# Graph layer on one core: one release for a chunk's gathers, two scatter matmuls, a transposed product tile, five key blocks on ScalarE

## The chip, the cores and the metric

The kernel runs on one core of a Trainium2 chip. The metric is device time in microseconds (us) of one execution. Three runs of the kernel before gave 1787.23, 1787.67 and 1792.86 us; their median is 1787.67 us. The engines are called as in the profile: PE is TensorE, DVE is VectorE, ACT is ScalarE, POOL is GpSimd, SP is SyncE, which issues most loads.

## The reference

One message-passing layer on a graph of 6250 nodes with 64 features and 206250 edges, sorted by destination. In short:

```python
h = maximum(layernorm(x), 0)
msg = relu(h[src] + edge_attr)                    # one row of 64 per edge
agg = segment_sum(msg, dst, 6250)
out = x + relu((h + agg) @ W1 + b1) @ W2 + b2
```

All is float32. The costly part is h[src], a gather of 206250 rows of 256 bytes, and the sum of the edges by destination.

## The kernel before

**Tiling.** The edges are cut into 124 chunks of 13 tiles of 128 edges (`TILES_PER_CHUNK` = 13). A partition holds 13 neighbouring edges of a chunk, and since edges are sorted, each partition's edges mostly have one or two destinations. Four chunks make a turn; there are 31 turns (t, with u = 0 to 3 for the chunk in it) and four sets of buffers (`SLOTS`). Turn 0 and the last three turns (`EARLY_TURNS`, 28 to 30) are written out; turns 1 to 27 are a loop on each engine, each engine with its own.

**Two ways to fetch h[src].** Of a chunk's 13 tiles, nine are fetched by POOL: `gather_rows` issues one indirect DMA a tile from `h_table` in DRAM (L361). The other four are made by PE (`pe_tiles`): `candidates` multiplies, for each tile, a one-hot matrix of keys (`keyhot`, seven key blocks) with the table of h, kept as two float16 halves. That is 14 matmuls of 128x448 a tile (L1050), into one of four PSUM banks, and it yields seven candidate rows for each edge. DVE masks them (L820) and sums over the seven (L826); this is `combine`.

**The keys.** The one-hot matrix of a chunk has seven key blocks. DVE makes `DVE_BLOCKS` = 3 of them (L710) and ACT four, each with an Abs (L617) and then one Relu over all four (L621). There are two `keyhot` buffers, so those of a chunk can be made once PE is done with the chunk two before it.

**The sum by destination.** For each chunk DVE runs three steps, laid between the masks of the following chunk (`segment_step`): `sum_edges` adds the gathered rows to the edge rows that ACT copied to PSUM (L856); `part_edges` applies relu and multiplies with a flag for each edge, once for the destination of the partition's first edge and once for that of its last (L865, 2 x 13 x 64 elements, into `parts`); `add_parts` sums over the 13 tiles (L875) into `ends`, two rows of 64 a partition. `scatter_ends` on PE multiplies these with a one-hot matrix of the place in a window of 64 nodes (L385), each end in two matmuls of 32 columns, and DVE adds the window to `agg` (L897). A float32 matmul shows as two records in the trace.

**Order and releases.** PE does two chunks of candidates and then the scatters of two earlier chunks. In the loop POOL gathers chunk c while PE makes the candidates of chunk c-2, and is held to its pace: `gather_chunk` passes `gather_rows` a list of releases, and before gathers 0, 2, 4 and 6 of a chunk POOL waits for the first, second, third and fourth candidate tile of chunk c-2:

```python
gather_rows(u, n, gathered[u], {i * n // m: pe_before(old_t, old_u, i) + 1 for i in range(m)})
```

Before that it waits for the chunk's indices and until `sum_edges` has read the buffer's former rows. SP loads keys, indices and edges for two chunks at a time, one pair ahead (`load_pair`); the edge loads (L492) mark the pairs in the trace. At the end `first_layer` and `second_layer` run the two dense layers (L411, L426) on finished groups of nodes.

Of the kernel before, what the change touches and what calls it, by code (L numbers as in the profile page):

```python
# [13 lines left out]
P = 128  # L14
D = 64
# [23 lines left out]
WIN = 64  # L39
AGG_COLS = MARGIN + NODES_PAD + WIN  # L40
BLOCK = 64
QUARTER = 32
ENDS = 2
SEGMENT_STEPS = 3
N_BLOCKS = NODES_PAD // BLOCK
# [36 lines left out]
assert PE_FIRST[-1] == PE_TILES[-1] and PE_MAX == max(*PE_FIRST, *PE_LAST[0], *PE_LAST[1], *PE_LAST[2])  # L82
CAND = GROUP
KEY_BLOCKS = N_GROUPS
DVE_BLOCKS = 3
CAND_BANKS = 4
F16 = mybir.dt.float16
BF16 = mybir.dt.bfloat16
# [78 lines left out]
def build(nc, x_rows, x_cols, src_t, src_keys, src_cands, dst_t, base_t, edges_t, w1, b1, w2, b2, out):  # L167
# [8 lines left out]
    with ExitStack() as ctx:  # L176
# [52 lines left out]
        edge = [edge_pair[u // PAIR][:, u % PAIR, :, :] for u in range(SLOTS)]  # L229
        gath = [sb(f"gath{u}", [P, TILES_PER_CHUNK, D]) for u in range(SLOTS)]  # L230

        parts = sb("parts", [P, ENDS, TILES_PER_CHUNK, D])
        msg = parts[:, 0, :, :]
        ends = [sb(f"ends{u}", [P, ENDS, D]) for u in range(SLOTS)]

        onehot = [sb(f"onehot{u}", [P, ENDS, WIN]) for u in range(SLOTS)]
# [118 lines left out]
        def gather_rows(u, tiles, signal, released=None):  # L355

            for r in range(tiles):
                if released is not None and r in released:
                    nc.gpsimd.wait_ge(cands_ready, released[r])
                    nc.gpsimd.sem_inc(slot_taken, 1)  # L360
                nc.gpsimd.indirect_dma_start(  # L361
                    out=gath[u][:, r, :], out_offset=None, in_=h_table,
                    in_offset=bass.IndirectOffsetOnAxis(ap=idx[u][:, r:r + 1], axis=0),
                ).then_inc(signal, 16)
# [16 lines left out]

        def scatter_ends(u, bank, signal):
            for k in range(ENDS):
                for d in range(0, D, QUARTER):
                    last = nc.tensor.matmul(bank[k * D + d:k * D + d + QUARTER, 0:WIN],  # L385
                                            ends[u][:, k, d:d + QUARTER], onehot[u][:, k, :], start=True, stop=True)
            last.then_inc(signal, 1)

        def scatter_strays(bank, signal):
# [130 lines left out]
        @block.gpsimd  # L520
        def _(pool):
            nc.gpsimd.iota(iota_i[:, :], [[1, P]], base=0, channel_multiplier=0).then_inc(iota_made, 1)
            nc.gpsimd.iota(iota_p[:, :], [[0, 1]], base=0, channel_multiplier=1).then_inc(iota_made, 1)

            nc.gpsimd.iota(key_iota_i[:, :], [[P, KEY_BLOCKS]], base=0, channel_multiplier=1).then_inc(iota_made, 1)

            pool.wait_ge(iota_made, 3)
            nc.gpsimd.memset(agg[D:2 * D, :], 0.0).then_inc(odd_half_zeroed, 1)  # L530
            pool.wait_ge(odd_half_zeroed, 1)

            for g in POOL_CENTRES:
                pool.wait_ge(mean_ready, g + 1)
                centre(nc.gpsimd, g).then_inc(centred_by_pool, 1)


            pool.wait_ge(h_stored, 16 * N_GROUPS)
            for u in range(SLOTS):
                pool.wait_ge(idx_loaded[u // PAIR], 16)  # L540
                gather_rows(u, pool_tiles(0, u), gathered[u])

            def gather_chunk(t, u):
                pool.wait_ge(idx_loaded[u // PAIR], t * 16 + 16)

                pool.wait_ge(summed, t * SLOTS + (u + 1 - SLOTS))

                old_t, old_u = back(t, u, 2)
                n, m = pool_tiles(t, u), pe_tiles(old_t, old_u)
                gather_rows(u, n, gathered[u], {i * n // m: pe_before(old_t, old_u, i) + 1 for i in range(m)})  # L550

            with pool.Fori(1, EARLY_TURNS[0]) as t:
                for u in range(SLOTS):
                    gather_chunk(t, u)
            for t in EARLY_TURNS:
                for u in range(SLOTS):
                    gather_chunk(t, u)

            pool.wait_ge(flag_ready, 1)
            flag = pool.value_load(outside_i[0:1, 0:1], min_val=0, max_val=P)  # L560
            with pool.If(flag > 0):
                with pool.Fori(0, N_CHUNKS) as c:
                    pool.wait_ge(g_free, c + 1)
                    pool.wait_ge(g_idx_loaded, c * 16 + 16)
                    pool.sem_inc(slot_taken, 1)
                    gather_rows(0, TILES_PER_CHUNK, g_gathered)
# [105 lines left out]
        def _(dve):  # L672
# [186 lines left out]
            def part_edges(t, u):  # L859

                dve.wait_ge(summed, t * SLOTS + u + 1)
                if u > 0 or not first(t):

                    dve.wait_ge(ends_ready, t * SLOTS + u)
                nc.vector.scalar_tensor_tensor(  # L865
                    out=parts[:, :, :, :],
                    in0=(edge_near if near(t) else edge_sum).unsqueeze(1).to_broadcast([P, ENDS, TILES_PER_CHUNK, D]),
                    scalar=0.0,
                    in1=side[:, bass.ds(t * SLOTS + u, 1), :, :].rearrange("p c k r -> p (c k) r").unsqueeze(3)
                    .to_broadcast([P, ENDS, TILES_PER_CHUNK, D]), op0=ALU.max, op1=ALU.mult).then_inc(parted, 1)  # L870

            def add_parts(t, u):

                dve.wait_ge(parted, t * SLOTS + u + 1)
                nc.vector.tensor_reduce(ends[u][:, :, :], parts[:, :, :, :].rearrange("p k r d -> p k d r"), AX_X,  # L875
                                        ALU.add).then_inc(ends_ready, 1)

            def segment_step(step, t, u):
                if step == 0:
# [298 lines left out]
```

## Time and profile before

| What | Value |
|---|---|
| Median of three runs | 1787.67 us |
| Profiled execution, its own time | 1790.81 us |
| Its span | 1789.0 us |
| Mean granted clock of TensorE | 0.922 |
| PE busy | 1500.4 us (84%) |
| DVE busy | 1450.7 us (81%) |
| ACT busy | 667.0 us (37%) |
| POOL busy | 1101.1 us (62%), 1125 gathers |
| DMA | mean 64 GB/s |

The page gives the busy time of each engine, the chain of work that ended last, and the groups of instructions by line. The timeline gives single instructions in order, with the idle time before them in brackets and what ended it. "issue" there means that the engine waited for nothing that the profile shows, "remote" another core or a queue that it doesn't know. Matmuls are pipelined: what counts is the distance from start to start. "DMA_INDIRECT" on POOL is the making of one gather's descriptors, not the transfer.

### The profile page before, as it was taken

Reading aid. Unit: us, or ns where it says so; the run is one execution under the profiler, and the core shown is the slowest. Engines: PE = TensorE matmul, PEld = TensorE weight load, DVE = VectorE, ACT = ScalarE, POOL = GpSimd, SP = SyncE. Lnnn points to the kernel's source line nnn. Section 1 sums busy time; section 2 is a strip of 40 time slices with the busy share of each in tenths; the row PEclk is TensorE's granted clock in tenths of the full one; section 3 lists DMA queues with packets and bytes.
Section 4 is the critical chain, followed back from the end, with each engine's and each line's share of the span. In section 5 each row is a group of like instructions: output and inputs, shape, how many; then the busy total and the mean of one; then the engine's idle time right before and its main releaser. Section 6 shows DMA issues by size and latency. Waiting matters only on the chain.

```text
span 1789.0 us, 25748 instructions
## 1 busy us (share of the span) xinstructions
PE 1500.4 (84%) x7987; PEld 729.6 (41%) x7987; DVE 1450.7 (81%) x2075; ACT 667.0 (37%) x759; POOL 1101.1 (62%) x1136
## 2 busy tenths in 40 slices
PE   4498898889888988988888989889889889889675
PEld 2143444344444434434444444444444344444332
DVE  8299888878878878888888888888888787889565
ACT  5033433343344334334433433344344334333221
POOL 4566666666666666666666566666666665667660
PEclk9699999999899999999999989999999899999796
DMA  5122222221221222212212212212222222122120
GB/s 202 25 72 49 70 72 58 61 71 48 72 71 48 72 70 49 72 48 71 72 48 72 71 47 72 71 48 72 64 55 72 48 72 71 47 72 74 45 59 21
DMA packets 67162, 115.15 MB, mean 64 GB/s; under 512 B 29810, under 2 KB 32882, under 8 KB 67010
## 3 DMA queue, kind: packets, MB, share of 16 engines
q1 hardware_dynamic: 30130, 75.86, 12.7%
q0 software_dynamic: 36000, 36.94, 10.6%
q10 hardware_dynamic: 1008, 2.06, 0.3%
q8 instruction: 12, 0.20, 0.0%
q14 instruction: 12, 0.10, 0.0%
HBM read 111.43 MB, written 3.34 MB: 64 GB/s over the span
## 4 chain that ended last, share of the span: by engine, by line
PE 66%; issue 15%; DVE 13%; another core or an unknown queue 4%; DVEq 1%; ACT 1%; POOL 0%; POOLq 0%
PE ps_cand L1050 63%; DVE picked L820 3%; DVE gath L826 3%; DVE ends L875 2%; DVE parts L865 2%; PE ps L385 2%; DVE keyhot L710 1%; PE ps_edge L411 1%; ACT agg L601 0%; DVEq L887 0%; PE ps_edge L426 0%; DVE key_iota L687 0%; DVE cand_mask L758 0%; DVE side L774 0%
## 5 line engine op out<-in xcount | busy, mean ns | idle before, releaser
L361 POOL DMA_INDIRECT gath<-h_table,idx_pair x1125 | 1092.3, 971 | 640.8 <-issue 328.1
L1050 PE MATMUL ps_cand<-table_hi,keyhot 128*128 128x448 f16 x3409 | 1252.0, 367 | 85.6 <-issue 78.1
L1050 PE MATMUL ps_cand<-table_lo,keyhot 128*128 128x448 f16 x3409 | 1250.0, 367 | 79.0 <-issue 78.5
L1050 PEld LDWEIGHTS ps_cand<-table_hi,keyhot 128*128 128x128 f16 x3409 | 344.0, 101 | 459.3 <-issue 170.4
L1050 PEld LDWEIGHTS ps_cand<-table_lo,keyhot 128*128 128x128 f16 x3409 | 343.9, 101 | 425.1 <-issue 149.7
L820 DVE TENSOR_TENSOR picked<-ps_cand,cand_mask 128x448 f32<-128x448 f32 x487 | 300.9, 618 | 265.0 <-remote 179.1
L608 ACT ACTIVATE ps_edge<-edge_pair 128x832 f32<-128x832 f32 x112 | 97.4, 869 | 799.7 <-DVE parts L865 559.7
L875 DVE TENSOR_REDUCE ends<-parts 128x128 f32<-128x1664 f32 x124 | 372.9, 3007 | 0.0
L617 ACT ACTIVATE keyhot<-key_pair,key_bias 128x512 f16<-128x512 f16 (+2 forms) x480 | 302.9, 702 | 182.0 <-remote 113.2
L826 DVE TENSOR_REDUCE gath<-picked 128x64 f32<-128x448 f32 x487 | 298.1, 612 | 4.1
L621 ACT ACTIVATE keyhot<-keyhot,hot_bias 128x2048 f16<-128x2048 f16 (+2 forms) x120 | 236.8, 1974 | 3.9
L865 DVE SCALAR_TENSOR_TENSOR parts<-ps_edge,side 128x1664 f32<-128x1664 f32 x112 | 210.6, 1881 | 0.7 <-issue 0.7
L710 DVE TENSOR_SCALAR keyhot<-key_pair,key_iota 128x512 f16<-128x512 f16 (+2 forms) x388 | 117.2, 359 | 0.2
L856 DVE TENSOR_TENSOR ps_edge<-gath,ps_edge 128x832 f32<-128x832 f32 x112 | 114.0, 1018 | 0.0
L385 PE MATMUL ps<-onehot,ends 128*32 128x64 f32 x992 | 48.6, 237 | 56.6 <-issue 55.3
L385 PEld LDWEIGHTS ps<-onehot,ends 128*32 128x32 f32 x992 | 26.4, 113 | 95.3 <-issue 91.6
L897 DVE TENSOR_TENSOR agg<-agg,ps 128x64 f32 x124 | 27.0, 217 | 42.0 <-DVE agg L897 22.1
L417 ACT ACTIVATE xh<-ps_edge,b_sb 64x448 f32<-64x448 f32 (+2 forms) x14 | 8.8, 629 | 116.6 <-PE ps_edge L411 108.3
L411 PE MATMUL ps_edge<-agg,w_sb 128*64 128x448 f32 (+2 forms) x28 | 19.6, 800 | 38.1 <-DVE x_sq L436 15.0
L838 DVE TENSOR_TENSOR onehot<-iota_f,place 128x128 f32<-128x128 f32 x124 | 35.2, 284 | 9.5 <-remote 7.4
L1025 PE MATMUL ps<-ident,xh 128*64 128x128 f32 x49 | 11.7, 417 | 26.1 <-DVE xh L741 21.7
L865 DVE SCALAR_TENSOR_TENSOR parts<-xh,side 128x1664 f32<-128x1664 f32 x12 | 22.6, 1880 | 0.0
(71 smaller groups left out, 156.9 us busy)
## 6 DMA issues: line engine op xcount, KB each, us to landing
edge_pair<-edges_t SPq DMA_DIRECT2D x62, 832.0 KB
gath<-h_table,idx_pair POOLq DMA_INDIRECT x1125
key_pair<-key_table SPq DMA_DIRECT2D x62, 256.0 KB
h_table<-xh SPq DMA_DIRECT2D x7, 224.0 KB, 2.5
x_b<-x_cols SPq DMA_DIRECT2D x1, 1568.0 KB
out<-x_sq SPq DMA_DIRECT2D x6, 224.0 KB
idx_pair<-src_t SPq DMA_DIRECT2D x62, 13.0 KB
xh<-x_rows ACTq DMA_DIRECT2D x4, 224.0 KB, 5.2
```

The costliest lines, as they stand in the source:

```text
L361: nc.gpsimd.indirect_dma_start(out=gath[u][:, r, :], out_offset=None, in_=h_table, in_offset=bass.IndirectOffsetOnAxis(ap=idx[u][:, r:r + ...
L385: last = nc.tensor.matmul(bank[k * D + d:k * D + d + QUARTER, 0:WIN], ends[u][:, k, d:d + QUARTER], onehot[u][:, k, :], start=True, stop=True)
L608: nc.scalar.activation(edge_near, edge[u], ACT.Copy).then_inc(edge_copied, 1)
L617: last = nc.scalar.activation(keyhot[u % 2][:, a, 0:n], key[u][:, P * PE_MAX - n:], ACT.Abs, bias=key_bias[:, a:a + 1])
L621: nc.scalar.activation(keyhot[u % 2][:, DVE_BLOCKS:, 0:n], keyhot[u % 2][:, DVE_BLOCKS:, 0:n], ACT.Relu, bias=hot_bias[:, 0:1], scale=-1.0 ...
L710: last = nc.vector.tensor_scalar(keyhot[u % 2][:, a, 0:n], key[u][:, P * PE_MAX - n:], key_iota[:, a:a + 1], 1.0 / SCALE, ALU.is_equal, AL ...
L820: nc.vector.tensor_tensor(picked[i][:, :, :], ps_cand[buf][:, 0:D * CAND].rearrange("p (d b) -> p d b", b=CAND), mask.to_broadcast([P, D, ...
L826: nc.vector.tensor_reduce(gath[u][:, pool_tiles(t, u) + i, :], picked[i][:, :, :], AX_X, ALU.add).then_inc(selected, 1)
L856: nc.vector.tensor_tensor(edge_near if near(t) else edge_sum, gath[u][:, :, :], edge_near if near(t) else edge[u], ALU.add).then_inc(summe ...
L865: nc.vector.scalar_tensor_tensor(out=parts[:, :, :, :], in0=(edge_near if near(t) else edge_sum).unsqueeze(1).to_broadcast([P, ENDS, TILES ...
L875: nc.vector.tensor_reduce(ends[u][:, :, :], parts[:, :, :, :].rearrange("p k r d -> p k d r"), AX_X, ALU.add).then_inc(ends_ready, 1)
L1050: last = nc.tensor.matmul(bank[:, 0:D * CAND], keyhot[u % 2][:, a, i * P:(i + 1) * P], half[:, a, :, :].rearrange("p d b -> p (d b)"), sta ...
```

## The change

Four things change. In `gather_rows` POOL waits only in front of gather 0 of a chunk, for the first candidate tile of chunk c-2; the three other waits and their increments of `slot_taken` go. `scatter_ends` issues one matmul of 64 columns for each end in place of two of 32. `parts` is laid out with the 13 tiles innermost, so `add_parts` reads contiguous elements; `part_edges` becomes two instructions, one for each end, each writing its elements 13 words apart. `DVE_BLOCKS` falls from 3 to 2, so ACT makes five key blocks.

```diff
--- before.py
+++ after.py
@@ -39,7 +39,6 @@
 WIN = 64
 AGG_COLS = MARGIN + NODES_PAD + WIN
 BLOCK = 64
-QUARTER = 32
 ENDS = 2
 SEGMENT_STEPS = 3
 N_BLOCKS = NODES_PAD // BLOCK
@@ -82,7 +81,7 @@
 assert PE_FIRST[-1] == PE_TILES[-1] and PE_MAX == max(*PE_FIRST, *PE_LAST[0], *PE_LAST[1], *PE_LAST[2])
 CAND = GROUP
 KEY_BLOCKS = N_GROUPS
-DVE_BLOCKS = 3
+DVE_BLOCKS = 2
 CAND_BANKS = 4
 F16 = mybir.dt.float16
 BF16 = mybir.dt.bfloat16
@@ -229,8 +228,8 @@
         edge = [edge_pair[u // PAIR][:, u % PAIR, :, :] for u in range(SLOTS)]
         gath = [sb(f"gath{u}", [P, TILES_PER_CHUNK, D]) for u in range(SLOTS)]
 
-        parts = sb("parts", [P, ENDS, TILES_PER_CHUNK, D])
-        msg = parts[:, 0, :, :]
+        parts = sb("parts", [P, ENDS, D, TILES_PER_CHUNK])
+        msg = parts[:, 0, :, :].rearrange("p d r -> p (d r)").rearrange("p (r d) -> p r d", d=D)
         ends = [sb(f"ends{u}", [P, ENDS, D]) for u in range(SLOTS)]
 
         onehot = [sb(f"onehot{u}", [P, ENDS, WIN]) for u in range(SLOTS)]
@@ -355,8 +354,8 @@
         def gather_rows(u, tiles, signal, released=None):
 
             for r in range(tiles):
-                if released is not None and r in released:
-                    nc.gpsimd.wait_ge(cands_ready, released[r])
+                if released is not None and r == 0:
+                    nc.gpsimd.wait_ge(cands_ready, released)
                     nc.gpsimd.sem_inc(slot_taken, 1)
                 nc.gpsimd.indirect_dma_start(
                     out=gath[u][:, r, :], out_offset=None, in_=h_table,
@@ -381,9 +380,8 @@
 
         def scatter_ends(u, bank, signal):
             for k in range(ENDS):
-                for d in range(0, D, QUARTER):
-                    last = nc.tensor.matmul(bank[k * D + d:k * D + d + QUARTER, 0:WIN],
-                                            ends[u][:, k, d:d + QUARTER], onehot[u][:, k, :], start=True, stop=True)
+                last = nc.tensor.matmul(bank[k * D:(k + 1) * D, 0:WIN], ends[u][:, k, :], onehot[u][:, k, :],
+                                        start=True, stop=True)
             last.then_inc(signal, 1)
 
         def scatter_strays(bank, signal):
@@ -546,8 +544,7 @@
                 pool.wait_ge(summed, t * SLOTS + (u + 1 - SLOTS))
 
                 old_t, old_u = back(t, u, 2)
-                n, m = pool_tiles(t, u), pe_tiles(old_t, old_u)
-                gather_rows(u, n, gathered[u], {i * n // m: pe_before(old_t, old_u, i) + 1 for i in range(m)})
+                gather_rows(u, pool_tiles(t, u), gathered[u], pe_before(old_t, old_u) + 1)
 
             with pool.Fori(1, EARLY_TURNS[0]) as t:
                 for u in range(SLOTS):
@@ -862,18 +859,18 @@
                 if u > 0 or not first(t):
 
                     dve.wait_ge(ends_ready, t * SLOTS + u)
-                nc.vector.scalar_tensor_tensor(
-                    out=parts[:, :, :, :],
-                    in0=(edge_near if near(t) else edge_sum).unsqueeze(1).to_broadcast([P, ENDS, TILES_PER_CHUNK, D]),
-                    scalar=0.0,
-                    in1=side[:, bass.ds(t * SLOTS + u, 1), :, :].rearrange("p c k r -> p (c k) r").unsqueeze(3)
-                    .to_broadcast([P, ENDS, TILES_PER_CHUNK, D]), op0=ALU.max, op1=ALU.mult).then_inc(parted, 1)
+                for k in range(ENDS):
+                    last = nc.vector.scalar_tensor_tensor(
+                        out=parts[:, k, :, :].rearrange("p d r -> p r d"), in0=edge_near if near(t) else edge_sum,
+                        scalar=0.0,
+                        in1=side[:, bass.ds(t * SLOTS + u, 1), k, :].rearrange("p c r -> p (c r)").unsqueeze(2)
+                        .to_broadcast([P, TILES_PER_CHUNK, D]), op0=ALU.max, op1=ALU.mult)
+                last.then_inc(parted, 1)
 
             def add_parts(t, u):
 
                 dve.wait_ge(parted, t * SLOTS + u + 1)
-                nc.vector.tensor_reduce(ends[u][:, :, :], parts[:, :, :, :].rearrange("p k r d -> p k d r"), AX_X,
-                                        ALU.add).then_inc(ends_ready, 1)
+                nc.vector.tensor_reduce(ends[u][:, :, :], parts[:, :, :, :], AX_X, ALU.add).then_inc(ends_ready, 1)
 
             def segment_step(step, t, u):
                 if step == 0:
```

## Rows read from the trace of the kernel before

**Rows 1.** The page, part 4: the chain of waits, by engine and by line.
```profile
PE 66%; issue 15%; DVE 13%; another core or an unknown queue 4%; DVEq 1%; ACT 1%; POOL 0%; POOLq 0%
PE ps_cand L1050 63%; DVE picked L820 3%; DVE gath L826 3%; DVE ends L875 2%; DVE parts L865 2%; PE ps L385 2%; DVE keyhot L710 1%; PE ps_edge L411 1%; ACT agg L601 0%; DVEq L887 0%; PE ps_edge L426 0%; DVE key_iota L687 0%; DVE cand_mask L758 0%; DVE side L774 0%
```

**Rows 2.** Timeline of SP: start us, us, engine, line, operation: edge loads.
```profile
102.27 0.33 SPq L492 DMA_DIRECT2D edge_pair<-edges_t  x1
...
1565.67 0.33 SPq L492 DMA_DIRECT2D edge_pair<-edges_t  x1
```

**Rows 3.** Timeline of PE around one stall; in brackets idle before, releaser.
```profile
813.74 0.35 PE L1050 MATMUL ps_cand<-table_hi,keyhot 128*128 128x448 f16 x1
813.93 0.35 PE L1050 MATMUL ps_cand<-table_lo,keyhot 128*128 128x448 f16 x1
...
815.99 0.35 PE L1050 MATMUL ps_cand<-table_lo,keyhot 128*128 128x448 f16 x1 [1.08 <-issue]
817.40 0.35 PE L1050 MATMUL ps_cand<-table_hi,keyhot 128*128 128x448 f16 x1 [1.06 <-issue]
818.10 0.54 PE L1050 MATMUL ps_cand<-table_lo,keyhot 128*128 128x448 f16 x1 [0.36 <-issue]
818.43 0.58 PE L1050 MATMUL ps_cand<-table_hi,keyhot 128*128 128x448 f16 x1
818.81 0.58 PE L1050 MATMUL ps_cand<-table_lo,keyhot 128*128 128x448 f16 x1
```

**Rows 4.** Timeline of PE: a scatter slot, and a second layer.
```profile
791.93 0.43 PE L385 MATMUL ps<-onehot,ends 128*32 128x64 f32 x16
792.29 0.36 PE L1050 MATMUL ps_cand<-table_hi,keyhot 128*128 128x448 f16 x1
...
1714.05 1.67 PE L426 MATMUL ps_edge<-w_sb,xh 65*128 65x64 f32 x14
```

**Rows 5.** Timeline of POOL: first and last gathers of two runs.
```profile
788.84 0.95 POOL L361 DMA_INDIRECT gath<-h_table,idx_pair  x1 [2.64 <-remote]
...
802.51 0.94 POOL L361 DMA_INDIRECT gath<-h_table,idx_pair  x1 [2.60 <-remote]
...
815.03 0.94 POOL L361 DMA_INDIRECT gath<-h_table,idx_pair  x1 [0.30 <-issue]
818.96 0.94 POOL L361 DMA_INDIRECT gath<-h_table,idx_pair  x1 [2.99 <-remote]
```

**Rows 6.** Timeline of PE and POOL at the start.
```profile
48.39 0.35 PE L1050 MATMUL ps_cand<-table_hi,keyhot 128*128 128x448 f16 x1 [0.18 <-issue]
...
74.92 0.95 POOL L361 DMA_INDIRECT gath<-h_table,idx_pair  x1 [0.30 <-issue]
...
79.19 0.53 PE L1050 MATMUL ps_cand<-table_lo,keyhot 128*128 128x448 f16 x1 [0.87 <-issue]
```

**Rows 7.** Waits: who waited for whom: us, times, longest us.
```profile
POOL gath L361 <- PE ps_cand L1050: 160.5, 84, 16.6
PE ps_cand L1050 <- issue: 156.5, 189, 2.5
POOL gath L361 <- remote: 140.7, 57, 3.6
```

**Rows 8.** Groups by shape: xcount, busy us, mean ns, idle before.
```profile
L875 DVE TENSOR_REDUCE ends<-parts 128x128 f32<-128x1664 f32 x124 | 372.9, 3007 | 0.0
L826 DVE TENSOR_REDUCE gath<-picked 128x64 f32<-128x448 f32 x487 | 298.1, 612 | 4.1
L617 ACT ACTIVATE keyhot<-key_pair,key_bias 128x512 f16<-128x512 f16 x456 | 291.0, 709 | 170.9 <-remote 113.2 <-PE ps_cand L1050 42.9 <-issue 14.7
L621 ACT ACTIVATE keyhot<-keyhot,hot_bias 128x2048 f16<-128x2048 f16 x114 | 228.2, 2002 | 3.7
L865 DVE SCALAR_TENSOR_TENSOR parts<-ps_edge,side 128x1664 f32<-128x1664 f32 x112 | 210.6, 1881 | 0.7 <-issue 0.7
L710 DVE TENSOR_SCALAR keyhot<-key_pair,key_iota 128x512 f16<-128x512 f16 x363 | 110.9, 362 | 0.2
```

## Prediction

> **What bounds the kernel now.** I read the chain of waits first. It shows TensorE (PE) holding 66% of the path, nearly all of it the candidate matmuls of L1050, and 15% as "issue", time in which PE waits for nothing that the profile names [rows 1]. So the question is how fast PE walks through its matmuls. The loop over turns 1 to 27 handles 54 pairs of chunks, and the edge loads on SP mark them: (1565.67 - 102.27) / 54 = 27.10 us a pair [rows 2]. A pair needs 112 candidate matmuls at 0.19 us start to start (813.74 to 813.93 [rows 3]), 21.2 us, and one slot of 0.36 us for its scatters (791.93 to 792.29 [rows 4]): 21.5 us. The missing 5.6 us are the "issue" time and the slow clock behind it.
>
> The timeline says where they come from. At 813.93 PE stops running at 0.19 us and takes 1.4 us a matmul (815.99, 817.40), with no semaphore named; at 818.10 it runs again, and its matmuls come 0.38 us apart for a while (818.43, 818.81), the pace of 1.2 GHz in place of 2.4, before they are fast again [rows 3]. Beside it stands GpSimd (POOL): it had issued eleven gathers 1.25 us apart without a break from 802.51, the last at 815.03, and then stood for 2.99 us until 818.96 [rows 5]. PE began to starve 11.4 us after that run began and recovered 2.1 us after its last gather ended (815.97 to 818.10). This repeats: I count 28 unbroken runs of eleven gathers and six of thirteen, nearly all with a stall of PE that ends 2.0 to 2.4 us after the run does. 32 runs have nine; the one at 788.84 is followed by a break of 2.6 us. The plainest case is at the start, where no wait ties the two. POOL issues 37 gathers without a break until 75.87; PE falls to 1.4 us a matmul from 48.39, with all its operands there, and runs on at 79.19 [rows 6]. So a long unbroken run of gathers starves PE of instructions, and only a break of POOL ends it.
>
> The breaks are made by the waits in gather_rows. POOL stood 160.5 us for PE's candidates by name and 140.7 us for "remote" [rows 7]; by position in a chunk, in turns 1 to 27, I get 53 us in front of gather 0 and 71, 91 and 41 us in front of gathers 2, 4 and 6, which the change takes away.
>
> The Trainium skill ("Runtime: NRT & Kernel Launch", "Instruction fetch mechanics") says that the sequencer fetches instructions over its own DMA queue in blocks and that this is mostly hidden. By that rule a run of gathers would do nothing to PE and the gathers' term would be 0, a sum of 1781 us or, with fewer PE instructions, the rival "faster" below. The trace disagrees with "hidden": PE stood with nothing named for 156.5 us in front of the candidate matmuls alone [rows 7].
>
> **The gathers at one release.** Chunk c waits once, for the first candidate tile of chunk c-2, and then issues nine gathers in 9 x 1.25 = 11.25 us. The next release comes when PE has done another 56 matmuls and half a scatter slot, 56 x 0.189 + 0.2 = 10.8 us if it isn't starved. Starvation starts about 11.4 us into a run. So a chunk's nine gathers end just after the next release is there, and POOL goes on without a break. Today it is caught at gather 2, whose release needs 14 matmuls more (13.4 us), so the run ends at eleven. After the change nothing stops it before the eighteenth, whose successor needs a release PE is far from. One cycle, from one run's start to the next, for two chunks (112 + 8 = 120 matmul records, since a pair's scatters fall from 16 to 8):
> - The run takes 17 x 1.25 + 0.95 = 22.2 us; PE is fed again at 22.2 + 2.1 = 24.3 us.
> - Fed stretch: I take 11.9 us instead of 11.4, as PE passes some 5% fewer instructions. (11.9 - 0.36) / 0.189 = 61 records.
> - Starved stretch: 24.3 - 11.9 = 12.4 us at 1.41 us = 9 records. (At the start it was as slow, or slower.)
> - Rest: 50 records, eight at 0.374 us on the slow clock and 42 at 0.189 us: 10.9 us, in which POOL stands.
> Together 35.2 us against 27.10: +8.1 us a pair. With PE fed the whole break, the next run finds it in the same state, so the pattern should hold. I let 48 of 54 pairs do it (the first turns run behind VectorE, and a run now and then will be broken after nine): 48 x 8.1 = +389 us. Bounds: in the timeline the stalls start between 9.3 us (run from 1301.5, after a short break) and 12.8 us (run from 873.2) into a run. With 9.3: 47 + 11 records by 24.3 us, 62 left, 13.2 us, so 37.5 us a pair, +10.4, times 54 = +562 us. With 12.8: 66 + 8, 46 left, 10.2 us, 34.5 us a pair, +7.4 a pair; if only half of the pairs do it, +200 us. Unrolled turns 28 to 30: POOL has gathers of 2.5 us among its own there, I take 0.
>
> **Two scatter matmuls of 64 columns.** Now 16 records of a pair share a slot of 0.36 us. Seven second-layer matmuls, full width, make 14 records in 1.67 us, 0.107 us each [rows 4], so the narrow ones run beside each other. Afterwards eight records are twice as wide. If they run two abreast the slot stays 0.4 us; one by one, 8 x 0.107 = 0.86 us, +0.5 us x 62 = +31 us; if the slot halves, -11 us. Nearest row is today's overlap: 0.
>
> **VectorE.** The sum over r (L875) takes 3.007 us for 1664 elements read 64 apart; L826 sums 448 contiguous ones in 0.612, and L865 passes 1664 in 1.881 [rows 8]. Between the last two lie 1.04 ns an element and 0.144 us fixed, so the contiguous sum is 1.88 us: -1.13 us a chunk. The product becomes two of 832 elements, 0.144 + 0.868 = 1.01 us each, +0.14 together, if writing 13 words apart costs nothing; at L875's slope, (3.007 - 0.144) / 1664 = 1.72 ns, they take 2 x 1.57 = 3.15 us, +1.27. One key block less: -0.30 us (L710 takes 0.362, the next starts 0.3 later). VectorE's sum: -1.3 to -0.2 us a chunk. It lies beside PE. L875 has only 2% of the path [rows 1], 36 us, of which 1.13 / 3.007 = 38% could go: 13 us, where VectorE leads at the start and in turns 28 on. I take -10; the bounds are -13 and 0.
> The Trainium skill ("Advanced Engine Details and Errata", "Memory Cachelines") says SBUF has 16-byte lines and an access that changes line each time pays. The 3.007 us of L875 agree. Applied to the new write, 52 bytes apart, it makes VectorE's gain close to nothing: the term would be 0 and the sum 10 us higher.
>
> **ScalarE.** One more key block, 0.61 of its 0.709 us, and a Relu over 2560 instead of 2048 elements, 2.002 x 1.25: +1.1 us a chunk [rows 8]. A chunk of ScalarE now takes 5.3 us (a copy of 0.87, four blocks of 0.61, the Relu of 2.0); at 13.5 us a chunk the rest is idle, and its keys are there some 4 to 9 us before PE turns to them. 0; if that cover were gone, 124 x 1.1 = +136 us.
>
> **Sum.** Profiled execution: span 1789.0, time 1790.8 us, 3.1 us over the median of 1787.67. 1790.8 + 389 + 0 - 10 + 0 = 2170; on the scale of the median 2167, say 2165 us.
>
> **Rivals.**
> - Half of it. Runs of nine stay where PE starves before the next release; today's 32 such runs speak for it, and a pair costs 27.1 us then. Against it: fewer PE instructions make the stall start later, and after a long break PE is full. With 24 of 54 pairs in runs of eighteen: +194 - 10, 1970 us.
> - Faster: the breaks of POOL are only the effect of PE's stall, which has its own cause in PE's instruction count. Then the change costs nothing on POOL and PE passes 496 of 7987 matmul records fewer, 6%. Stalls and the slow clock behind them take 5.6 x 54 = 302 us; 6% is 19 us, and VectorE's 10 more: 1760 us. It decides if POOL's run does not set the end of a stall. For it: the stall frees POOL's own wait. Against: the fixed 2.1 us behind the last gather, and 37 gathers at the start with no wait in between.
> - No change: POOL's saved breaks come back as one longer break before gather 0, as long in sum, with stalls as today and VectorE's gain hidden: 1788 us.
> - That the change doesn't do what it says: the 54 pairs could run with breaks at gather 0 of 2 to 3 us each, as at 788.84 to 802.51, 13.7 us a chunk. This is the case of no change again.
>
> **Chances.** Runs of eighteen in most pairs, 2165 us: 0.62, own range 2060 to 2270. Half of it, 1970: 0.19. Faster, 1760: 0.12. No change: 0.04. The remaining 0.03 is a small loss, 1800 to 1880, by scatters in single file or wide writes. A measurement tells a change of 0.3% (5 us). Faster 0.12, same 0.04, slower 0.84. The range from 1880 to 2280 us leaves out the two small cases and the far ends.
>
> **What would show it.** Right: runs of eighteen gathers 1.25 us apart, breaks of some 12 us before gather 0 and none elsewhere; PE at 1.4 us a matmul for 10 to 13 us in each pair, ending 2 us after a run; edge loads 35 us apart; PE's mean granted clock below today's. The scatter slot at 0.4 us; L875 at 1.9 us; the two products at 1.0 us each if the write is free, 1.6 if not. Wrong: PE at 0.19 us a matmul in the second half of a run of eighteen, or pairs at 27 us with runs of nine.

## The result and the profile after

The changed kernel takes 1872.24 us (median of four runs, 1865.08 to 1887.71) against 1787.61 us for the kernel before (four runs, 1787.23 to 1792.86): ratio 1.047, 95% interval 1.0441 to 1.05. It is slower, as forecast, but by 85 us and not by 377, and outside the range. ("Fed" means below that PE's matmuls start 0.19 us apart, or 0.38 at the slow clock; "starved" that they start 1.4 to 2.8 us apart with no wait named.) The profiled execution has a span of 1863.1 us, its own time is 1865.08 us, and TensorE's mean granted clock is 0.905 (before 0.922).

The page after, part 4, the chain of waits: PE and "issue" hold 89% of it, 81% before [rows 1].

```profile
PE 72%; issue 17%; DVE 8%; another core or an unknown queue 2%; ACT 1%; DVEq 0%; POOL 0%; POOLq 0%
```

Timeline of SP after, the edge loads that answer to [rows 2]:

```profile
102.01 0.33 SPq L490 DMA_DIRECT2D edge_pair<-edges_t  x1
...
1640.76 0.33 SPq L490 DMA_DIRECT2D edge_pair<-edges_t  x1
```

(1640.76 - 102.01) / 54 = 28.50 us a pair, against 27.10. The loop costs 54 x 1.40 = 75 us more, the start and the end together 1 us less: all of the profiled execution's 74 us lies in the loop.

Timeline of POOL after: first and last gather of a run of nine, then the same of a run of eighteen, then the next run.

```profile
844.64 0.94 POOL L360 DMA_INDIRECT gath<-h_table,idx_pair  x1 [2.85 <-PE ps_cand L1047]
...
854.63 0.94 POOL L360 DMA_INDIRECT gath<-h_table,idx_pair  x1 [0.30 <-issue]
858.21 0.94 POOL L360 DMA_INDIRECT gath<-h_table,idx_pair  x1 [2.64 <-remote]
...
879.49 0.94 POOL L360 DMA_INDIRECT gath<-h_table,idx_pair  x1 [0.30 <-issue]
889.58 0.95 POOL L360 DMA_INDIRECT gath<-h_table,idx_pair  x1 [9.15 <-PE ps_cand L1047]
```

Timeline of PE beside that run of eighteen, which answers to [rows 3] and [rows 4]:

```profile
838.34 0.35 PE L1047 MATMUL ps_cand<-table_lo,keyhot 128*128 128x448 f16 x1
...
860.85 0.45 PE L383 MATMUL ps<-onehot,ends 128*64 128x64 f32 x8
861.23 0.36 PE L1047 MATMUL ps_cand<-table_hi,keyhot 128*128 128x448 f16 x1
...
869.95 0.35 PE L1047 MATMUL ps_cand<-table_hi,keyhot 128*128 128x448 f16 x1
870.25 0.35 PE L1047 MATMUL ps_cand<-table_lo,keyhot 128*128 128x448 f16 x1
872.35 0.35 PE L1047 MATMUL ps_cand<-table_hi,keyhot 128*128 128x448 f16 x1 [1.75 <-issue]
875.16 0.53 PE L1047 MATMUL ps_cand<-table_lo,keyhot 128*128 128x448 f16 x1 [2.46 <-issue]
...
882.16 0.53 PE L1047 MATMUL ps_cand<-table_hi,keyhot 128*128 128x448 f16 x1 [1.57 <-issue]
883.57 0.55 PE L1047 MATMUL ps_cand<-table_lo,keyhot 128*128 128x448 f16 x1 [0.87 <-issue]
883.91 0.58 PE L1047 MATMUL ps_cand<-table_hi,keyhot 128*128 128x448 f16 x1
...
888.44 0.35 PE L1047 MATMUL ps_cand<-table_lo,keyhot 128*128 128x448 f16 x1
```

The stall is the one forecast: it begins 12.0 us after the run (870.25 against 858.21) and ends 3.1 us after the last gather (883.57 against 880.43). In it PE passes one matmul every 1.4 to 2.8 us. All 18 runs of eighteen in the loop show it: it begins 11.4 to 16.0 us after the run's start and ends 1.5 to 3.2 us after the last gather. Counted over the loop, POOL makes only two kinds of run: 72 of nine gathers (13.76 us on average from one start to the next) and 18 of eighteen (30.93 us, 29.78 to 32.11). Before, a pair took 27.10 us. So the eighteens cost 18 x (30.93 - 27.10) = 69 us, and the nines 72 x (13.76 - 13.55) = 15 us at most (they also carry the two ends of the stretch).

Waits after, which answer to [rows 7]:

```profile
PE ps_cand L1047 <- issue: 243.6, 264, 2.5
POOL gath L360 <- PE ps_cand L1047: 239.8, 51, 16.8
POOL gath L360 <- remote: 63.8, 25, 3.7
```

PE's nameless idle time grew from 156.5 to 243.6 us: 87 us, the size of the loss. POOL's waits by name and "remote" are 304 us, as before (301), but some waits of the kernel after stand under "issue", whose longest rose from 3.3 to 9.0 us. Counted by position in the loop, POOL's idle times of over 0.5 us grew from 305 to 373 us, and all of them now stand in front of gather 0.

Groups of the page after, which answer to [rows 8] (shapes, count, busy us, mean ns):

```profile
L618 ACT ACTIVATE keyhot<-keyhot,hot_bias 128x2560 f16<-128x2560 f16 (+2 forms) x120 | 287.2, 2393 | 3.9
L863 DVE SCALAR_TENSOR_TENSOR parts<-ps_edge,side 128x832 f32<-128x832 f32 x224 | 338.6, 1590 | 0.0
L873 DVE TENSOR_REDUCE ends<-parts 128x128 f32<-128x1664 f32 x124 | 232.4, 1874 | 0.0
```

### The profile page after: what moved, and what is told of

Read it like the earlier page. It is cut to its first block, busy times and chain, and to the rows that moved or that the text cites. A ratio compares the mean times of both kernels' runs of the same rounds, so it can differ in the third digit from the quotient of the medians.

```text
span 1863.1 us, 24304 instructions
## 1 busy us (share of the span) xinstructions
PE 1491.0 (80%) x7491; PEld 722.8 (39%) x7491; DVE 1407.4 (76%) x2079; ACT 788.0 (42%) x879; POOL 1092.2 (59%) x1136
## 4 chain that ended last, share of the span: by engine, by line
PE 72%; issue 17%; DVE 8%; another core or an unknown queue 2%; ACT 1%; DVEq 0%; POOL 0%; POOLq 0%
PE ps_cand L1047 69%; DVE parts L863 2%; PE ps L383 2%; DVE picked L817 1%; DVE gath L823 1%; DVE ends L873 1%; PE ps_edge L409 1%; PE ps_edge L424 1%; DVE keyhot L707 0%; ACT agg L598 0%; DVE key_iota L684 0%; DVEq L884 0%; DVE cand_mask L755 0%; DVE row_sum L722 0%
## 5 line engine op out<-in xcount | busy, mean ns | idle before, releaser
L614 ACT ACTIVATE keyhot<-key_pair,key_bias 128x512 f16<-128x512 f16 (+2 forms) x600 | 375.1, 700 | 144.9 <-remote 81.8
L863 DVE SCALAR_TENSOR_TENSOR parts<-ps_edge,side 128x832 f32<-128x832 f32 x224 | 338.6, 1590 | 0.0
L618 ACT ACTIVATE keyhot<-keyhot,hot_bias 128x2560 f16<-128x2560 f16 (+2 forms) x120 | 287.2, 2393 | 3.9
L873 DVE TENSOR_REDUCE ends<-parts 128x128 f32<-128x1664 f32 x124 | 232.4, 1874 | 0.0
L707 DVE TENSOR_SCALAR keyhot<-key_pair,key_iota 128x512 f16<-128x512 f16 (+2 forms) x268 | 84.8, 361 | 0.2
L383 PE MATMUL ps<-onehot,ends 128*64 128x64 f32 x496 | 41.9, 253 | 53.2 <-issue 52.3
L383 PEld LDWEIGHTS ps<-onehot,ends 128*64 128x64 f32 x496 | 28.6, 151 | 89.5 <-issue 88.4
L835 DVE TENSOR_TENSOR onehot<-iota_f,place 128x128 f32<-128x128 f32 x124 | 35.2, 284 | 11.0 <-remote 11.0
L863 DVE SCALAR_TENSOR_TENSOR parts<-xh,side 128x832 f32<-128x832 f32 x24 | 36.4, 1595 | 0.0
```

Of the source, the lines that this page charges most:

```text
L383: last = nc.tensor.matmul(bank[k * D:(k + 1) * D, 0:WIN], ends[u][:, k, :], onehot[u][:, k, :], start=True, stop=True)
L614: last = nc.scalar.activation(keyhot[u % 2][:, a, 0:n], key[u][:, P * PE_MAX - n:], ACT.Abs, bias=key_bias[:, a:a + 1])
L618: nc.scalar.activation(keyhot[u % 2][:, DVE_BLOCKS:, 0:n], keyhot[u % 2][:, DVE_BLOCKS:, 0:n], ACT.Relu, bias=hot_bias[:, 0:1], scale=-1.0 ...
L707: last = nc.vector.tensor_scalar(keyhot[u % 2][:, a, 0:n], key[u][:, P * PE_MAX - n:], key_iota[:, a:a + 1], 1.0 / SCALE, ALU.is_equal, AL ...
L863: last = nc.vector.scalar_tensor_tensor(out=parts[:, k, :, :].rearrange("p d r -> p r d"), in0=edge_near if near(t) else edge_sum, scalar=0.0,
L873: nc.vector.tensor_reduce(ends[u][:, :, :], parts[:, :, :, :], AX_X, ALU.add).then_inc(ends_ready, 1)
```

## The experiments

**Two conditions.** The kernel before itself ran at two speeds, by session: about 1789 us in the sessions of the first result, of the first four experiments and of the g runs, and about 1533 us in those of e5 to e8, of the f runs, the h runs and i1. Within a session it kept to one (1783 to 1794, or 1531 to 1535). Chip number 5 was met in both (1788.72, later 1532.29), so the number of the chip doesn't decide it. I call them the starving and the fed condition; every ratio is within one session. What sets the condition is open.

### Which edit costs

e1 is the kernel before with nothing but the single release. e2 is the changed kernel with the four releases back:

```diff
-                if released is not None and r == 0:
-                    nc.gpsimd.wait_ge(cands_ready, released)
+                if released is not None and r in released:
+                    nc.gpsimd.wait_ge(cands_ready, released[r])
```

e3 is the kernel before with the scatters of 64 columns alone:

```diff
-                for d in range(0, D, QUARTER):
-                    last = nc.tensor.matmul(bank[k * D + d:k * D + d + QUARTER, 0:WIN],
-                                            ends[u][:, k, d:d + QUARTER], onehot[u][:, k, :], start=True, stop=True)
+                last = nc.tensor.matmul(bank[k * D:(k + 1) * D, 0:WIN], ends[u][:, k, :], onehot[u][:, k, :],
+                                        start=True, stop=True)
```

and e4 with the transposed `parts`, the two products and the contiguous sum alone (the third and the last hunk of the change).

> The kernel before with only the releases changed: POOL waits once a chunk, in front of gather 0. Theory (long unbroken runs of gathers starve PE): in the loop POOL's runs have nine or eighteen gathers and nothing between; each eighteen costs 3 to 4 us over two nines (30.9 against 27.1 us), and the time is 1840 to 1885 us. With more PE instructions a chunk than in the changed kernel, PE starves earlier and there are rather fewer runs of eighteen. Rival (the loss comes from the other edits: wide writes, scatters or ScalarE's fifth block): 1783 to 1793 us, no change.

> The changed kernel with the four releases of a chunk put back; scatters, layout and five key blocks on ScalarE stay. Theory: no run of eighteen, pairs of 27 us as before, and something of the 6% fewer PE instructions: 1765 to 1790 us. Rival (the other edits carry the loss): 1850 us or more.

> The kernel before with one scatter matmul of 64 columns for each end in place of two of 32; nothing else. Theory: 496 fewer matmul records on PE, so PE starves a little later in each run of gathers: 1770 to 1788 us. Rival (the wide scatters no longer run beside each other): up to 0.5 us more a pair, 1788 to 1820 us.

> The kernel before with only the product tile transposed: two products with writes 13 words apart, one contiguous sum. From the trace of the changed kernel the products cost 2 x 1.59 us in place of 1.88 and the sum 1.87 in place of 3.01, so VectorE gains 0.2 us or less a chunk, off the path: 1783 to 1792 us, no change. Rival (VectorE's order sets the path: ScalarE's copy waits for the products, which now end 1.3 us later): 1795 to 1830 us.

Measured, kernel before 1788.91 us:

| Kernel | us | Ratio, 95% |
|---|---|---|
| e1 one release | 1877.29 | 1.0504 [1.048, 1.0529] |
| e2 change, old releases | 1772.84 | 0.9902 [0.9878, 0.9927] |
| e3 scatters of 64 | 1778.88 | 0.9936 [0.9915, 0.9957] |
| e4 layout | 1787.02 | 0.9999 [0.9982, 1.0017] |

The single release is the whole loss, 5.0%; the other three edits gain 1.0%, of which the scatters 0.6%, the layout nothing; the rest is no larger than the intervals. e1 shows the same two kinds of run as the change, 78 of nine and 15 of eighteen (31.48 us each).

### Is it the unbroken run?

If so, any break of POOL must feed PE again, even one that adds work. g1 (also run as e6 and f3) is the changed kernel, single release and all, with a memset on POOL in the middle of each chunk from turn 1 on:

```diff
+                if idled is not None and r == 5:
+                    nc.gpsimd.memset(pool_idle[:, :], 0.0).then_inc(pool_idled, 1)
```

g2 (also e5, f2) is the kernel before with five gathers a chunk in place of nine in turns 0 to 27 (six in the first chunk); it leaves out the rows of the other gathers, so its output isn't the layer's.

```diff
-                n, m = pool_tiles(t, u), pe_tiles(old_t, old_u)
+                n, m = sent(t, u), pe_tiles(old_t, old_u)
```

g3 (also e7, f4) is e2 with releases in front of the gathers of chunks 2 and 3 of turn 0 too, where POOL issues 37 gathers without a break [rows 6]:

```diff
-                gather_rows(u, pool_tiles(0, u), gathered[u])
+                n, m = pool_tiles(0, u), pe_tiles(0, u - 2)
+                gather_rows(u, n, gathered[u],
+                            {i * n // m: pe_before(0, u - 2, i) + 1 for i in range(m)} if u >= 2 else None)
```

> The changed kernel with a memset on POOL between gathers 4 and 5. Where the kernel before takes 1789 us. Theory (a break between gathers feeds PE): 1735 to 1760 us, no stall of PE over 5 us in the loop. Rival (only the releases pace PE): 1900 us or more. Where the kernel before takes 1533 us: 1738 us again, POOL the bound.

> The kernel before with five gathers a chunk. Where the kernel before takes 1789 us. Theory: 1530 to 1560 us, no stall of PE in the loop. Rival (the stalls are PE's own): 1700 us or more. Where the kernel before takes 1533 us: 1531 us again.

> The three other edits with four releases a chunk, and releases also for the chunks 2 and 3 of turn 0. Where the kernel before takes 1789 us. Theory: 1755 to 1768 us. Rival (turn 0 ends by POOL or VectorE anyhow): 1770 to 1776 us. Where the kernel before takes 1533 us: 1499 us again.

Measured in the starving condition, kernel before 1788.72 us: g1 1761.36 us, 0.9848 [0.9831, 0.9866]; g2 1549.56 us (one run, its profile a span of 1547.7); g3 1765.45 us, 0.9876 [0.9857, 0.9895]. g1 lies 1.4 us above the range expected of it, g2 and g3 lie in theirs.

g1 against the changed kernel adds 270 us of work to POOL and is 6% faster by the ratios (0.985 against 1.047). Its loop has 105 runs of nine gathers, nearly all from one memset to the next, 13.47 us apart, and PE stands for 6.4 us at most at one go (13.9 in the changed kernel); its nameless idle time in front of the candidates is 51.4 us in place of 243.6. The timelines of its POOL and its DVE at the same moment:

```profile
801.47 0.94 POOL L365 DMA_INDIRECT gath<-h_table,idx_pair  x1 [0.30 <-issue]
802.41 2.25 POOL L364 MEMSET pool_idle<- 128x2560 f32 x1
804.83 1.06 POOL L365 DMA_INDIRECT gath<-h_table,idx_pair  x1 [0.17 <-POOL pool_idle L364]
```

```profile
802.38 2.69 DVE L713 TENSOR_SCALAR keyhot<-key_pair,key_iota 128x512 f16<-128x512 f16 x2
804.99 0.61 DVE L823 TENSOR_TENSOR picked<-ps_cand,cand_mask 128x448 f32<-128x448 f32 x1
```

So it is not the wait for PE that feeds PE, but that POOL issues no gather for a while: the rival by which PE's stalls have their own cause falls here. g1 alone leaves a doubt, since its memset slows DVE too (below) and PE waits 167.9 us for DVE's masks. g2 has no memset in its loop and PE's full instruction count, and stands only 17.6 us on "issue" in front of the candidates (156.5 before); it can't tell breaks from fewer gathers, which g1 can. g3 shows it at the start: with POOL held after 56.13, PE is fed again at 59.63 rather than 79.19. Its PE, after the last gather of that run ended at 57.07:

```profile
48.41 0.35 PE L1050 MATMUL ps_cand<-table_hi,keyhot 128*128 128x448 f16 x1 [0.29 <-issue]
...
58.91 0.53 PE L1050 MATMUL ps_cand<-table_hi,keyhot 128*128 128x448 f16 x1 [0.88 <-issue]
59.63 0.53 PE L1050 MATMUL ps_cand<-table_lo,keyhot 128*128 128x448 f16 x1 [0.19 <-issue]
```

Of the 20 us that the start stall is shorter, little is left at the end: g3's ratio lies 0.0026 under e2's, 5 us, less than the two intervals tell apart.

### The same kernels where PE is fed

e5, e6, e7 and a kernel with two releases a chunk (e8) ran in the fed condition, and so did f1, the changed kernel itself, with f2 to f4. e8's edit against the changed kernel:

```diff
-                gather_rows(u, pool_tiles(t, u), gathered[u], pe_before(old_t, old_u) + 1)
+                n, m = pool_tiles(t, u), pe_tiles(old_t, old_u)
+                gather_rows(u, n, gathered[u], {0: pe_before(old_t, old_u, 0) + 1, n // 2 + 1: pe_before(old_t, old_u, 2) + 1 if m > 2 else pe_before(old_t, old_u, 1) + 1})
```

> The kernel before with fewer gathers: five a chunk in turns 0 to 27 (six in the first chunk) in place of nine or ten; the rest of the rows is left out. PE's and VectorE's work and all waits are as before. Theory (runs of gathers starve PE): five gathers take 6.3 us of a chunk's 11, POOL breaks for over 2 us in each chunk, PE's stalls in the loop vanish, a pair takes 22 to 24 us and the time is 1550 to 1650 us. Rival (the stalls belong to PE's own instruction count): stalls every 110 to 130 matmuls as before, pairs of 27 us, 1750 us or more.

> The changed kernel, still with one release a chunk, and a memset of 2560 columns of a spare tile on POOL between gathers 4 and 5 of each chunk from turn 1 on: about 2.2 us in which POOL is busy but makes no gather. Theory (a break between gathers is what PE needs, whatever POOL does in it and whoever it waits for): PE never stands for long, no stall of 10 us is left, and POOL sets the pace at 11.25 + 2.5 = 13.8 to 14.2 us a chunk: 1790 to 1850 us, faster than the changed kernel (1872) although POOL has more to do. Rival (the releases were what paced PE, by their semaphores): the stalls stay and POOL's work comes on top, 1900 us or more.

> The changed kernel with the four releases (1772.84 us), and the same releases in turn 0 for the chunks 2 and 3, which now go without any. Theory: the run of 37 gathers at the start, in which PE starved from 48 to 79 us, is broken, PE gets through turn 0 some 20 us earlier, and POOL comes to its first wait in the loop 3 to 5 us later than now: 1755 to 1768 us. Rival (turn 0 ends by POOL or VectorE anyhow): 1770 to 1776 us.

> The changed kernel with two releases a chunk: in front of gather 0 for the first candidate tile of chunk c-2, in front of gather 5 for its third. Theory: gather 5 waits for a tile that a fed PE gives 5.5 us after the first, while POOL comes to it after 6.3 us; a starved PE holds POOL there. A run can then have 14 gathers, not 18: pairs of 27.2 to 28 us, 1775 to 1810 us, between the four releases (1773) and one (1872). Rival (only the wait in front of gather 2 catches POOL, since it comes first after the start of PE's stall): as with one release, 1850 us or more.

> The changed kernel itself, beside the kernel before on the same chip. The last four kernels ran on a chip on which the kernel before took 1532.72 us in place of 1789, with no stall of PE although POOL gathered without a break. Theory (the loss is PE's starvation behind runs of gathers, and that depends on the chip): where the kernel before takes 1789 us, the ratio is 1.045 to 1.05 as before; where it takes 1533, PE doesn't starve, eighteen gathers in a row cost nothing, and the change is faster by about 2% (1495 to 1510 us), as its form with two releases was. Rival (the single release costs something else than PE's starvation): slower than the kernel before on either chip.

| Kernel (before: 1532.72; f: 1533.13) | us | Ratio, 95% |
|---|---|---|
| f1 the change itself | 1499.98 | 0.9788 [0.9773, 0.9803] |
| e8 two releases | 1499.64 | 0.9782 [0.9767, 0.9797] |
| e7, f4 start releases | 1501.44, 1499.08 | 0.9786, 0.9783 |
| e6, f3 memset | 1737.72, 1738.23 | 1.1332, 1.1337 |
| e5, f2 five gathers | 1530.53, 1532.97 | one run each |

Here the change is 2.1% faster (interval 0.9773 to 0.9803), and how many releases a chunk has makes no difference. What two releases do in the starving condition was not measured. The timeline of f1's POOL shows why the term is gone: gathers 1.25 us apart right through the releases, each there in time.

```profile
598.40 0.94 POOL L360 DMA_INDIRECT gath<-h_table,idx_pair  x1 [0.30 <-issue]
...
607.14 0.95 POOL L360 DMA_INDIRECT gath<-h_table,idx_pair  x1 [0.30 <-PE ps_cand L1047]
608.39 0.94 POOL L360 DMA_INDIRECT gath<-h_table,idx_pair  x1 [0.30 <-issue]
```

and the page's part 4 for f1 has another bound, DVE (busy 94% of a span of 1496.3 us):

```profile
DVE 42%; PE 27%; issue 25%; DVEq 6%; ACT 1%; POOL 0%; POOLq 0%
```

f1's PE, in the middle of a run of gathers that never ends, is not slowed. From its timeline at the start, where the kernel before stalls from 48.39:

```profile
48.29 0.35 PE L1047 MATMUL ps_cand<-table_lo,keyhot 128*128 128x448 f16 x1
48.48 0.35 PE L1047 MATMUL ps_cand<-table_hi,keyhot 128*128 128x448 f16 x1
...
54.53 0.35 PE L1047 MATMUL ps_cand<-table_hi,keyhot 128*128 128x448 f16 x1
```

The two conditions together price the starvation, roughly, since they are different sessions: 1789 - 1533 = 256 us for the kernel before, 1872 - 1500 = 372 for the change, but 1761 - 1738 = 23 with the memset and 17 to 19 with five gathers. The change costs 116 us more there and saves 33 us otherwise: 83 us, about the loss.

**What is held up.** That the gathers keep instructions from PE is a reading that the traces don't bear out. In the trace before, the queues of kind "instruction" carry no packet from 190 to 1590 us, nearly the whole loop with its stalls, and none from 44 to 90 us, where the stall of the start lies. And the signals of PE are late too, before its matmuls are. The last matmul of the second candidate tile and DVE's mask of that tile, which waits for no other engine's work, in the trace before:

```profile
43.70 0.35 PE L1050 MATMUL ps_cand<-table_lo,keyhot 128*128 128x448 f16 x1
63.11 0.62 DVE L820 TENSOR_TENSOR picked<-ps_cand,cand_mask 128x448 f32<-128x448 f32 x1 [17.22 <-remote]
```

and the same two in f1:

```profile
43.37 0.35 PE L1047 MATMUL ps_cand<-table_lo,keyhot 128*128 128x448 f16 x1
45.81 0.62 DVE L817 TENSOR_TENSOR picked<-ps_cand,cand_mask 128x448 f32<-128x448 f32 x1
```

DVE stood idle for 17.22 us for a tile whose matmuls had run at full pace, 4.7 us before PE slowed at 48.39. Of the 487 increments of this semaphore (`cands_ready`) the trace of f1 has 486 within 0.25 us of a tile's end; the trace after has 206 so, and 206 more come 1.0 to 3.5 us after a gather ended, in POOL's breaks. So both PE's matmuls and its signals stand while POOL gathers. What they share with the gathers is open. The starving traces also lack records of increments (after, 297 of the masks' 487; f1, all), and every timed run here has a recorded span, so whether the recording takes part is open too.

> The changed kernel with a memset on POOL between gathers 4 and 5 again; on the chip where PE doesn't starve it took 1737.72 us, POOL being the bound at some 13.8 us a chunk. Theory: where the kernel before takes 1789 us, this one takes 1735 to 1760 us, since the memset gives PE its break: faster than the changed kernel (1872) and than the kernel before, with more work on POOL. Rival (only releases pace PE): 1900 us or more there.

> The other three edits with the four releases, and the same releases for the chunks 2 and 3 of turn 0, again; where PE doesn't starve it took 0.9786 of the kernel before. Theory: where the kernel before takes 1789 us: 1755 to 1768 us, 5 to 18 us less than without the releases in turn 0 (1772.84). Rival: 1770 to 1776 us.

The memset's 13% here was put down to POOL alone in the expectation of e6. The groups show a second cost, on DVE. Key blocks of f1 and then of g1, by the same view:

```profile
L707 DVE TENSOR_SCALAR keyhot<-key_pair,key_iota 128x512 f16<-128x512 f16 (+2 forms) x268 | 87.4, 371 | 0.2
```

```profile
L713 DVE TENSOR_SCALAR keyhot<-key_pair,key_iota 128x512 f16<-128x512 f16 (+2 forms) x268 | 336.0, 1296 | 0.2
```

DVE's key block waits for POOL's memset to end: in the pair of timelines above it began at 802.38 and ended at 805.07, the memset ran from 802.41 to 804.66. 248.6 us of DVE's time go there, nearly the memsets' 270. The Trainium skill ("SBUF — State Buffer", "Who interferes with whom") says that DVE in its faster modes and GpSimd share one port pair under an exclusive lock; this trace agrees. DVE's largest other groups are as long with the memset as without (masks 0.612 and 0.615 us, reductions 0.606 and 0.608); two groups of two small instructions beside the one memset at the start are longer (0.26 to 1.31 us, 0.20 to 1.38).

### A shorter break, and both together

h1 is g1 with the start releases; h2 and i1 are h1 with half the memset:

```diff
-        pool_idle = sb("pool_idle", [P, 2560])
+        pool_idle = sb("pool_idle", [P, 1280])
```

> The changed kernel with a memset of 2560 columns on GpSimd (2.25 us) between the fifth and the sixth gather of each chunk from turn 1 on, and with the old kind of release (one for each candidate tile of the chunk two before) in front of the gathers of chunks 2 and 3 of turn 0. Theory (TensorE starves behind a long unbroken run of gathers, and any break of 2 us or more ends the run): the break gave 0.985 and the start releases some 7 us (0.9876 against 0.9902), so together 0.981 of the kernel before, 1754 us, where the kernel before takes 1789. Where the kernel before takes 1533 TensorE does not starve, GpSimd has 9 x 1.25 + 2.4 = 13.7 us a chunk to do and sets the pace: 1.13 as before. Rival (the start's stall is paid again later, since VectorE leads the first turns): no better than the memset alone, 0.985.

> The same with a memset of 1280 columns, about 1.13 us by the 2.25 us of 2560. In the kernel before a stall of TensorE ended 2.0 to 2.4 us after the last gather of a run. Theory that a break must be that long from the last gather's end: a break of 0.3 + 1.13 us, 1.4 us, is too short, a run goes on through it, and the loop falls back into long runs with stalls of 10 us and more: 1.03 to 1.06 of the kernel before where that takes 1789 us. Rival (the share of POOL's time that is not gathers decides, or any other instruction between gathers is enough): no long stalls, and with less work on GpSimd the time is that of the long memset or lower, 0.965 to 0.985. Where the kernel before takes 1533 us: GpSimd has 12.6 us a chunk, and the time is 1.03 to 1.07.

> The kernel with the memset of 1280 columns and the start releases once more. Where the kernel before takes 1533 us: 1.053 as before. Where it takes 1789 us the theory that a break must last some 2 us from the last gather's end gives long runs and stalls of 10 us and more, 1.03 to 1.06; the rival (any instruction between gathers is enough) gives 0.965 to 0.985 and no long stalls.

All three fell into the fed condition: h1 1737.32 us, 1.1339 [1.1324, 1.1355]; h2 1613.65 us, 1.053 [1.0516, 1.0545]; i1 1614.4 us, 1.0529 [1.0512, 1.0547]. They confirm the price of the memset, 2.0 us a chunk for the long one and 1.0 for the short one ((1735.0 - 1496.3) / 120 and (1611.8 - 1496.3) / 120, spans against f1). How short a break may be where PE starves was not measured and stays open.

## Why the prediction was wrong in size

**Right.** The bound, that long runs of gathers hold it up, the sign, and which edit carries it. A run of eighteen lasts 22.2 us, as forecast. The fed stretch was taken as 11.9 us and is 12.0 at 870.25, PE is fed again 25.4 us after the run's start where I had 24.3, and the breaks stand in front of gather 0 alone, 8.7 us behind an eighteen where I had 12. The slot of the scatters is 0.38 us (860.85 to 861.23; forecast 0.4), the contiguous sum 1.874 us (forecast 1.88).

**Wrong: "I let 48 of 54 pairs do it".** There were 18. No eighteen ever follows another; they come after two or three nines, and in three places after eight, nine and fourteen. The reason lies in the second wrong term.

**Wrong: a cycle of 35.2 us.** It was 30.93. I charged PE with a pair's 120 matmul records in each cycle, 50 of them after the run. Eight were charged twice: the scatters' slot of 0.36 us was taken off the fed stretch, but their eight records were left among the 50. With 42 the rest is 9.4 us and the cycle 33.7, which explains 1.5 of the 4.3 us. In the cycle at 858.21 PE did 68 records before the stall, 6 in it and 23 after, 97 in all; over the 18 cycles 98.5 on average, and 65.7 over a nine. So an eighteen ends before PE has paid for it, and the nines after it make up what is missing. The same fact keeps eighteens apart: the run after one starts early with respect to its next release, ends at nine and waits. Per eighteen the cost is 30.93 - 27.10 = 3.8 us, not 8.1, and 18 x 3.8 = 69 us stands where 48 x 8.1 = 389 stood. Why the run after a stall starts so early the trace after shows: its release comes 0.8 us after the tile's last matmul ended (888.44 + 0.35 to 889.58; 0.77 to 0.80 us in all 18), while behind a nine the signal is late, 5.3 us in the median of 71 waits (838.34 + 0.35 to 844.64 is 5.95). 4.5 us are worth some 24 records of 0.19 us. That this lag is what keeps eighteens apart is argued from times; no run isolated it.

**The rival "half of it"** had the nearer count (24 of 54) and the same wrong price: 1970 us. With 3.8 us a pair it would have given 24 x 3.8 = 91 us, about what was seen.

**The terms at rest.** Scatters, 0 taken, -11 us the lower bound: e3 gave 0.6%, 10 us, its interval 8 to 15; the slot is no smaller (0.38 us), so the gain may come from PE having 496 records fewer to pass, which the forecast used for the stall's onset and priced at nothing here. VectorE, -10 taken: the product came out at the upper bound, 1.590 us (bound 1.57), so the wide write costs what the wide read did; 2 x 1.590 - 1.881 = +1.30 us against the sum's -1.13, and e4 measured no change. The rule on 16-byte lines in the Trainium skill ("Advanced Engine Details and Errata", "Memory Cachelines") gave just that term, 0, and these traces agree. ScalarE, 0: e2 holds it and is faster, as forecast; what the moved key block is worth alone no run shows.

**The fetch.** The Trainium skill ("Runtime: NRT & Kernel Launch", "Instruction fetch mechanics") calls fetching "mostly hidden". The prediction took PE's 156.5 us of nameless idle time as a sign against it, and a run of gathers as starving PE "of instructions". That step isn't shown: in the loop the trace has no instruction packet, so those stalls say nothing against the page. The forecast needed only that a run holds PE up, which holds in the starving condition. In the fed one the sum without the gathers' term has the right sign (f1 is 2.1% faster), and the forecast's sign would have been wrong. The profile before could tell only of its own condition, and the forecast was for that.

## What to carry over

Before loosening a wait, ask what its breaks give to the other engines: here they kept TensorE going, and dropping three of four cost 5% with no engine gaining work. Idle time without a name is not yet a cause: see whether the engine's signals are late too, and whether the queue that is blamed carries anything. When a stall is priced per cycle, count what the bound engine really does in that cycle; what it owes can be paid in the next ones, and that also limits how often the stall can return. Time a tuned kernel in several sessions: this one is 17% apart with nothing changed, and the change has the other sign there.

## What was not expected of the hardware

- The kernel before took 1789 us or 1533 us by session, and the traces of the starving sessions show TensorE held up beside GpSimd's gathers, those of the fed ones don't. What sets the condition is open.
- A TensorE held up beside a run of eighteen gathers passes a matmul every 1.4 to 2.8 us, and runs on 1.5 to 3.2 us after the last gather ended; with a GpSimd memset of 2.25 us between gathers it stands 51 us in place of 244.
- Its signals are late as well: VectorE's mask of the second tile began at 63.11 us for a matmul of 43.70 us.
- The same memset holds VectorE's float16 key blocks up, from 0.37 to 1.30 us on average.
